# Six shared feed-forward blocks of a macaron layer, woven in halves between the expert tiles

## The reference

```python
x = x + 0.5 * ffn(layernorm(x))
x = x + attention(layernorm(x))
x = x + 0.5 * ffn(layernorm(x))

def ffn(x):                                   # x: [8192, 128]
    scores = x @ router                       # 8 experts; the best 2 of each row are kept
    gates = sigmoid(scores of the best two, 0 elsewhere)
    for e in range(8):                        # an expert sees x * gate
        h = silu((x * gates[e]) @ w_in[e]) * ((x * gates[e]) @ w_swiglu[e])     # 256 hidden
        out += h @ w_out[e]
    out += (silu(x @ w_in_shared.T) * (x @ w_swiglu_shared.T)) @ w_out_shared.T  # the shared part
```

## Time and profile before

| | |
|---|---|
| median of 3 runs | 1043.9 us (1043.36 to 1047.52) |
| profiled execution | 1050.66 us, span of its instructions 1048.9 us |
| TensorE busy | 858.7 us, 82% of the span |
| VectorE, ACT, GpSimd busy | 642.4, 553.5, 678.2 us |
| TensorE's granted clock, mean | 0.91 |
| DMA | 88.01 MB, mean 84 GB/s |

### The profile page before, as it was taken

One profiled execution on the slowest core, in us unless ns is written; L12 is line 12 of the kernel. 1 busy time (PEld: TensorE's weight loads), 2 busy tenths in 40 slices (PEclk: granted clock), 3 DMA queues, 4 the chain that ended last, 5 costly groups with the idle time before them and its releaser, 6 DMA issues.

```text
span 1048.9 us, 19476 instructions
## 1 busy us (share of the span) xinstructions
PE 858.7 (82%) x5857; PEld 741.6 (71%) x5857; DVE 642.4 (61%) x2022; ACT 553.5 (53%) x1662; POOL 678.2 (65%) x733
## 2 busy tenths in 40 slices
PE   4665775669889888929999999986798989889898
PEld 3554664559788888814777777765697988788787
DVE  6645574636455554516889998875454545545586
ACT  3212331226555655539888888862265656655432
POOL 4867776747667666763388887677266666667651
PEclk9678787779999999969999999997698989999989
DMA  9511111242233323143022211111522322332494
GB/s 231 172 39 46 44 42 37 69 89 80 82 85 92 88 82 92 59 120 98 15 77 75 63 53 37 37 39 52 103 69 83 87 83 84 86 89 69 129 259 122
DMA packets 112921, 88.01 MB, mean 84 GB/s; under 512 B 13427, under 2 KB 102133, under 8 KB 112821
## 3 DMA queue, kind: packets, MB, share of 16 engines
q1 hardware_dynamic: 94816, 51.08, 19.0%
q0 software_dynamic: 17280, 35.69, 10.3%
q10 hardware_dynamic: 724, 0.01, 0.0%
HBM read 43.68 MB, written 43.04 MB: 83 GB/s over the span
## 4 chain that ended last, share of the span: by engine, by line
PE 60%; DVE 10%; ACT 10%; another core or an unknown queue 9%; issue 7%; DMA 2%; POOL 2%; SPq 0%; ACTq 0%; DVEq 0%
PE bank L931 12%; PE bank L915 6%; PE bank L1395 5%; PE bank L913 5%; PE bank L914 5%; PE bank L1371 4%; PE bank L921 4%; PE bank L1381 2%; ACT XG L869 2%; PE bank L724 2%; ACT SG L888 2%; ACT PR L1246 2%; POOL results L841 2%; PE bank L206 1%
## 5 line engine op out<-in xcount | busy, mean ns | idle before, releaser
L841 POOL DMA_INDIRECT results<-YO,XS x284 | 305.9, 1077 | 166.1 <-ACT YO L880 94.0
L822 DVE TENSOR_TENSOR HT<-bank,SG 128x512 f32<-128x512 f32 x142 | 98.2, 691 | 187.1 <-PE bank L915 75.5
L913 PE MATMUL bank<-XSH,WX 128*128 128x256 f32 x568 | 175.9, 310 | 2.7 <-issue 2.7
L1021 POOL DMA_INDIRECT pairs<-PAY,POS x128 | 135.5, 1059 | 63.3 <-issue 32.9
L414 POOL DMA_INDIRECT pairs<-PAY,POS x128 | 126.2, 986 | 65.1 <-DVE POS L241 35.3
L914 PE MATMUL bank<-XSL,WX 128*128 128x256 f32 x568 | 163.3, 287 | 1.1 <-issue 1.0
L915 PE MATMUL bank<-XSH,WX 128*128 128x256 f32 x568 | 163.2, 287 | 1.0 <-issue 0.9
L931 PE MATMUL bank<-WOE,HT 128*128 x1136 | 158.5, 284 | 0.1
L931 PEld LDWEIGHTS bank<-WOE,HT 128*128 128x128 f32 x1136 | 142.2, 196 | 4.4 <-issue 1.0
L869 ACT ACTIVATE XG<-XS 128x128 f32<-128x128 f32 x284 | 113.6, 401 | 19.3 <-DMA XS<-pairs 19.3
L888 ACT ACTIVATE SG<-bank 128x512 f32<-128x512 f32 x142 | 85.1, 599 | 55.4 <-PE bank L915 44.2
(11 more groups left out here) (197 smaller groups left out, 1793.1 us busy)
## 6 DMA issues: line engine op xcount, KB each, us to landing
XS<-pairs SPq DMA_DIRECT2D x142, 130.0 KB
Y<-results SPq DMA_DIRECT2D x32, 256.0 KB
YF<-results SPq DMA_DIRECT2D x32, 256.0 KB, 4.1
results<-YO,XS POOLq DMA_INDIRECT x284
pairs<-PAY,POS POOLq DMA_INDIRECT x256
out<-X SPq DMA_DIRECT2D x16, 256.0 KB, 3.1
pairs<-pad_rows SPq DMA_DIRECT2D x16, 130.0 KB
pairs<-pad_rows SPq DMA_DIRECT2D x1, 1040.0 KB
```

Source lines behind the costliest of these rows:

```text
L841: pool.indirect_dma_start(results, bass.IndirectOffsetOnAxis(ap=XS[:, u, j, AT_DEST:AT_DEST + 1].bitcast(U32), axis=0), YO[:, u, j, :], No ...
L913: pe.matmul(ps, WX[:, i % 2, 1, w], hi, start=True, stop=False)
L1021: pool.indirect_dma_start(pairs, bass.IndirectOffsetOnAxis(ap=POS[:, b % AB, j, c:c + 1], axis=0), PAY[:, b % AB, c, j, :], None).then_inc ...
```

## The change

In the second expert stage only (`experts(1)`, so `ffn` = 1), twelve more places are put into the list of tiles. Each is a half: 256 rows of one of the six blocks 3 to 8, computed with the shared weights. With 71 tiles and 12 halves the stage has ALL = 83 places; a half comes about every 5.5 tiles, the last ahead of the last five tiles. Buffers and PSUM banks now go by the place n and no longer by the tile i, except the banks of the transposes.

A half has no load, no scaling, no transpose, no weight copy and no scatter: ACT rounds 256 columns of `XTR` directly, VectorE subtracts, TensorE does the same twelve up matmuls of 256 columns with `SHH` and `SHL` and the same down matmuls with `WOS`, and VectorE adds half of the result to two of the block's four row groups (`half_add`). In the last stage the shared part begins with block 9 (`LATE` = 9), so that it has seven blocks instead of thirteen, and the loop on VectorE adds three results after a step instead of two.

```diff
+    WOVEN = 6
+    LATE = EARLY + WOVEN
...
+                halves = 2 * WOVEN if ffn else 0
+                ALL = NT + halves
+                past = NT * ffn
+                gap = NT / (halves + 1)
+                tile_at, half_at = [], []
+                for i in range(NT):
+                    if len(half_at) < halves and i >= gap * (len(half_at) + 1):
+                        half_at.append(len(tile_at))
+                        tile_at.append(None)
+                    tile_at.append(i)
+                def half_of(n):
+                    return EARLY + half_at.index(n) // 2, half_at.index(n) % 2
+                def half_x(n):
+                    b, h = half_of(n)
+                    return XTR[:, W * b + 2 * P * h:W * b + 2 * P * (h + 1)]
...
+                    def half_add(n):                                            # VectorE
+                        b, h = half_of(n)
+                        dve.wait_ge(k["e_down"], past + n + 1)
+                        half = X[:, BT * b + 2 * h:BT * b + 2 * h + 2, :]
+                        dve.scalar_tensor_tensor(out=half, in0=bank[6 + n % 2][:, 0:2 * D].rearrange("p (j d) -> p j d", d=D),
+                                                 scalar=0.5, in1=half, op0=ALU.mult, op1=ALU.add)\
+                           .then_inc(k["half_added"], 1)
...
-                    for i in range(-2, NT):
+                    for i in range(-2, ALL):
                         if 0 <= i:
...
+                            product(i)
+                        if i + 3 < ALL and not is_half(i + 3):
+                            no.ahead(tile_at[i + 3])
+                        if i + 2 < ALL:
+                            low(i + 2)
+                            if i + 2 and not is_half(i + 2):
                                 weights(i + 2)
...
+                        if 0 <= i - 1 and is_half(i - 1):
+                            half_add(i - 1)
...
+                    def high(n):                                                # ACT
+                        if is_half(n):
+                            b, h = half_of(n)
+                            act.wait_ge(k["xt_copied"], NB * ffn + b + 1)
+                            if n >= 2:
+                                act.wait_ge(k["e_up1"], past + n - 1)
+                            act.activation(XSH[:, n % 2, :], half_x(n), ACT.Copy).then_inc(k["xs_high"], 1)
...
+                    for i in range(-2, ALL + 1):                                # TensorE
+                        if 0 <= i < ALL:
                             up(i)
...
+                        if i + 2 < ALL and not is_half(i + 2):
                             turn(i + 2)
+                        if 0 <= i - 1 < ALL:
                             down(i - 1)
...
-                pe_shared(pe, EARLY, NB, KH, KL, HID)
+                pe_shared(pe, LATE, NB, KH, KL, HID)
...
-                    if b >= EARLY:
-                        dve.wait_ge(k["shared_added"], NB + b + 1)
+                    if b >= LATE:
+                        dve.wait_ge(k["shared_added"], NB - WOVEN + b + 1)
+                    elif b >= EARLY:
+                        dve.wait_ge(k["half_added"], 2 * (b - EARLY + 1))
...
-                for i in range(EARLY - 1, NB):
-                    dve_shared_step(dve, i, EARLY, NB, KH, KL, SSG, HID)
-                    while ahead < NB and (ahead < EARLY or ahead <= i) and (ahead < 2 * (i - EARLY) or i == NB - 1):
+                for i in range(LATE - 1, NB):
+                    dve_shared_step(dve, i, LATE, NB, KH, KL, SSG, HID)
+                    while ahead < NB and (ahead < LATE or ahead <= i) and (ahead < 3 * (i - LATE) or i == NB - 1):
```

More of the change, by code:

```diff
@@ L718, in pe_shared @@
                 if i >= lo:
-                    pe.wait_ge(k["hid0"], NB + i + 1)
-                    pe.wait_ge(k["hid1"], NB + i + 1)
-                    pe.wait_ge(k["shared_added"], NB + i)
+                    pe.wait_ge(k["hid0"], NB - WOVEN + i + 1)
+                    pe.wait_ge(k["hid1"], NB - WOVEN + i + 1)
+                    pe.wait_ge(k["shared_added"], NB - WOVEN + i)
                     for j in range(BT):
@@ L755, in dve_shared_step @@
             if lo <= i < hi:
-                dve.wait_ge(k["down"], NB + i + 1)
+                dve.wait_ge(k["down"], NB - WOVEN + i + 1)
                 dve.scalar_tensor_tensor(out=x_block(i), in0=bank[6][:, :].rearrange("p (j d) -> p j d", d=D),
@@ L922, in turn, with down @@
                         mm.then_inc(k["xs_turned"], 1)
-                    def down(i):
-                        e = no.expert(i)
-                        pe.wait_ge(k["e_hid"], done + i + 1)
-                        if i >= 2:
-                            pe.wait_ge(k["e_out"], done + i - 1)
+                    def down(n):
+                        e = None if is_half(n) else no.expert(tile_at[n])
+                        pe.wait_ge(k["e_hid"], past + n + 1)
+                        if n >= 2 and is_half(n - 2):
+                            pe.wait_ge(k["half_added"], halves_to(n - 2))
+                        elif n >= 2:
+                            pe.wait_ge(k["e_out"], done + tile_at[n - 2] + 1)
                         for j in range(2):
                             for c in range(FC):
-                                mm = pe.matmul(chunk(bank[6 + i % 2], j),
-                                               HT[:, i % 2, (2 * c + j) * P:(2 * c + j + 1) * P],
-                                               WOE[:, ds(e * FC * D + c * D, D)], start=(c == 0), stop=(c == FC - 1))
+                                w = WOS[:, c, :] if is_half(n) else WOE[:, ds(e * FC * D + c * D, D)]
+                                mm = pe.matmul(chunk(bank[6 + n % 2], j),
+                                               HT[:, n % 2, (2 * c + j) * P:(2 * c + j + 1) * P],
+                                               w, start=(c == 0), stop=(c == FC - 1))
                         mm.then_inc(k["e_down"], 1)
                     no.ahead(0)
-                    for i in range(-2, NT + 1):
-                        if 0 <= i < NT:
+                    for i in range(-2, ALL + 1):
+                        if 0 <= i < ALL:
                             up(i)
-                            if i + 1 < NT:
-                                no.ahead(i + 1)
-                        if i + 2 < NT:
+                            if i + 1 < ALL and not is_half(i + 1):
+                                no.ahead(tile_at[i + 1])
+                        if i + 2 < ALL and not is_half(i + 2):
                             turn(i + 2)
-                        if 0 <= i - 1 < NT:
+                        if 0 <= i - 1 < ALL:
                             down(i - 1)
```

108 lines of the change are left out of this document (59 added, 49 removed).

## The result

The changed kernel took 1034.0 us, the kernel before in the same comparison 1043.2: ratio 0.9928 (0.9905 to 0.9951), 16 runs each. But the sign belongs to the chip.

| | kernel before | changed kernel | ratio |
|---|---|---|---|
| chip 11 | 1041.0 | 1037.0 | 0.9950 (0.9914 to 0.9986) |
| chip 8 | 1069.8 | 1060.4 | 0.9927 (0.9893 to 0.9961) |
| chip 7 | 940.7 | 954.8 | 1.0148 (1.0125 to 1.0170) |

A forecast was written before the change was run, and what follows sets the result against it. TensorE was taken to bound the second expert stage, transfers the changed last stage. First load +30 us (28 + 4 - 2) and last stage -14 gave +16, 1060 us on the runs' median; range 1043 to 1071 us.

The forecast's parts named there:

- Step 1: Second expert stage: twelve halves at 2.33 us each on TensorE, which has no free time in steady stretches, +28 us.
- Step 2: Second expert stage: 40 us lost in spells grow with the added work, between -2.4 and +6.2 us, taken as +4.
- Rival A: Second expert stage: halves fill the lost time, the stage grows by 6 us only, 1036 us; chance 0.14.
- Step 2's guess at a cause: Second expert stage: fourteen 16 KB instruction-queue packets, one per about five tiles, may tie spells to TensorE's instructions.
- Step 3: Second expert stage: the halves' ACT and VectorE work lies beside TensorE's 2.33 us; cost nothing, at most 2 us.
- rival C: Second expert stage: VectorE's new wait isn't met, each half opens a 1.5 to 2 us spell, 1080 us; chance 0.08.
- Step 4: End of second expert stage: GpSimd's late scatters catch up during halves, 0 to -5 us, taken as -2.
- Step 5: Last stage: seven blocks for thirteen, but the transfers stay; 49 us instead of 63, -14 us.
- The term of 12.58 MB at 290 GB/s: Last stage: 32 loads and 16 stores of 256 KB at the earlier trace's rate take 43.4 us.

The follow-up runs named there:

- no_scatter: Kernel before without the second expert stage's scatters, SP waiting for ACT's outputs instead: 1018.3 us against 1069.8 on chip 8, ratio 0.9540.
- halves_added: Changed kernel with halves added at factor 0 and the last stage still doing all thirteen blocks: 968.5 us on chip 7, ratio 1.0283 to the kernel before.
- The two parts alone: Changed kernel with halves at factor 0 and all thirteen blocks, or without halves and blocks 3 to 8: 1.0263 and 0.9829 of the kernel before, chip 3.
- three woven blocks: Changed kernel with six halves instead of twelve, ten blocks in the last stage, two additions after a step: 1061.2 us on chip 12, ratio 0.9919.

## Why the prediction was wrong

*Step 1, twelve halves on TensorE, +28.* Right as the work's own size: 2.32 us in the chain, 28.0 us of stage on chip 7, +24.7 to +27.8 in time. Wrong as its effect on the chips with spells, because the two sentences "in the steady stretches TensorE has no free time for them" and "+28" forgot that a fifth of the stage was not steady.

*Step 2, the spells, +4.* This step failed, and with it the sum. The 40 us of lost time were read rightly, but treated as a cost that goes with the work, when added work made them smaller. I allowed for the half only 2.4 us of relief, the average share of the transposes' wait, "12 of 83 places". Terms 1 and 2 together were put at +32 and came out at +9.6 in the first pair of traces and +1.0 in the pair on chip 8; with the halves' own +28 the spells' term was -18 and -27 instead of +4. Whether halves meet spells at more than average places stays open: ten of the thirteen long intervals ended with a half in the first trace, 6 of 15 on chip 8, where 12 of 83 places would give 2. Part of it is the clock: 0.95 to 0.99 in the first pair, 0.94 to 0.99 in the second. Each 0.01 below 1 is 2% of the time at 1.2 GHz in place of 2.4, so some 8% of 222 us, 18 us, went from the lower level to the higher, worth at most 9 us in the first pair; an estimate, from the shares alone.

*Rival A* named the outcome (stage +6 against +9.6, 1036 us against 1034) and got 0.14. The reason that was held against it, that the down matmuls ahead of the half want a product which waits for the same late signal, is true for one tile; but in the spell shown, the inputs of the half's up matmuls, of a tile's down matmuls and of the next up matmuls had been got ready on signals from before the gap, so TensorE lost 0.75 us where VectorE lost 3.08. What a half does there that a tile would not was not isolated.

*Step 2's guess at a cause* (instruction blocks) fell: the packets are as many without spells (14 in the stage of no_scatter, as in the earlier trace rows; 51 in the whole of the changed kernel on quiet chip 7). The Trainium skill (Runtime: NRT & Kernel Launch, "Instruction fetch mechanics") has such crossings mostly hidden, and these runs agree.

*Step 3, the other engines, 0.* Right: no wait of VectorE's half addition for its down matmuls is listed in the changed kernel's stage (first trace, chip 8 and chip 7); rival C did not happen.

*Step 4, GpSimd's lateness, -2.* Right in kind on the chips with spells: from ACT's last output's end to the last scatter's end it was 7.3 us and is 3.9. On chip 7 nothing: the first load of results follows TensorE's first matmul of the last stage by 7.1 us with no halves and with them.

*Step 5, the last stage, -14.* The mechanism was right, the size off by 3: -17.2, -14.9 and, on chip 7, -16.0 (60.0 us in halves_added, 43.9 in the change). The term of 12.58 MB at 290 GB/s was mis-sized. The DMA view of chip 7's changed kernel, 908 to 952 us in 40 slices, stands at 335 to 346 in most of its second half:

```profile
GB/s 0 194 300 286 258 324 313 305 227 332 303 248 336 313 339 317 272 318 316 333 346 345 336 346 338 335 346 339 345 345 340 346 343 345 345 224 226 12 227 0
```

So the rate of the earlier trace rows was not the most that these transfers can do, as I took it. What held them to 290 in the kernel before, with six more blocks beside them, no run isolates. The Trainium skill (DMA: Bandwidth & Descriptors, the table under "Specifications") gives about 358 GB/s, from which a stage of 40 to 41 us was estimated beside the sum; 346 comes near to it, and the 44 to 46 us measured lie between the two. TensorE was no bound, and the additions waited for the loads, as forecast:

```profile
POOL YF L1574 <- DMA YF<-results: 21.6, 16, 5.2
...
DVE X L1593 <- POOL YF L1574: 12.1, 9, 1.6
```

*What stays open.* What of a scatter makes the spells, and how it reaches signals from TensorE: on a chip with spells only "all scatters or none" was tried. Whether added work fills the spells or makes them rarer (S or T). Why three chips have spells and three have none. Why in the first changed trace the remaining spells fall where halves run (before they came mostly every 4 to 6 tiles, halves come every 5 or 6, but a like period does not give the place). The two parts alone were measured on quiet chips only, so on the others the halves' cost is a reading of traces (+1 to +10 us of stage), and three woven blocks were not run on a quiet chip.

## What to carry to other kernels

Ask of lost time in a stage whether it is a cost that grows with the work or room that work can use: list the intervals of the bounding engine one by one, and look at what it has ready to do in a long one. A quick measure is filler, plain work of that engine and of no other: here 28 us of it cost 10 on a chip with lost time and 26 on one without. Where there is room, spread the pieces; in a row they found none of it. And compare on several chips before a change of under 2% is kept: this one is worth -0.7% or +1.5% by the chip, and a kernel without its lost time would be better than either.

## What the runs showed of the hardware

One and the same program took 941 to 945 us on three chips and 1041 to 1070 on three others, a difference of over 10%. In the second expert stage it is 184 us against 222 to 230. On the slower chips signals of finished matmuls came late in spells: ACT acted on one 2.95 us after the matmuls' recorded end (at 837.12), and in that spell TensorE's semaphores showed no count for 3.6 us and then six within 0.4. In the first trace, with two indirect DMAs for each tile, 18 of 70 tile intervals were over 3 us, where a steady one is 2.54; with no indirect DMA in the stage the same chip kept TensorE busy for 182.5 of 183 us. TensorE's mean granted clock in the stage of the kernel before was 0.94 to 0.95 with spells and 0.98 without; with the halves it was 0.99 on the chips with spells. Transfers of 256 KB between HBM and SBUF, loads and stores mixed, held 335 to 346 GB/s on one core for over ten microseconds.
